# Two attention layers in a fused kernel: score maxima run twelve steps ahead of the exponentials, not sixteen

## The chip, the cores and the metric

One core of one Trainium2 chip runs the whole program. The metric is device time in microseconds (us), from a few executions. Below, TensorE is PE in the rows, VectorE DVE, ScalarE ACT, GpSimd POOL, and SyncE SP. SP issues nearly all the DMAs of the layers concerned.

## The reference, cut to what matters

Eight sequences (batches) of 512 tokens, width 256, go through eight layers: four attention layers and four routed expert layers, each added to its input. Two of the attention layers are changed, "rope" (the second) and "latent" (the fourth). Both are 16-head attention with head size 16 and rotary embedding:

```
q = q * cos + rotate_half(q) * sin
k = k * cos + rotate_half(k) * sin
scores = einsum('bqhd,bkhd->bhqk', q, k) * scale
attn = softmax(scores, axis=-1)
out = einsum('bhqk,bkhd->bqhd', attn, v)
return out.reshape(b, l, d) @ Wo
```

In rope q, k and v come from one projection; in latent k and v go through a width of 128, and q is the normalised input itself.

## The kernel before, in words

Both layers are built by one function, `mha_pairs` (line 2001), over the whole layer's batches (NB = 8). The softmax needs each row's maximum before it can take exponentials, and the exponentials are made on scores that are laid out the other way round (keys on the partitions). So every score is computed twice: once as "top" (`max_scores`, line 2282), from which VectorE takes row maxima (`maxima`, line 2497), and once as "exp" (`exp_scores`, line 2296), from which ScalarE takes exponentials (line 2426). The maxima of a group of four heads are split into two 16-bit rows each, turned (`split_maxima`, line 2505), written by SP to DRAM (`write_rows`, line 2206) and loaded back as two extra rows of the query tile (`load_rows`, line 2213). The exp matmul of that group contracts over them too, and so subtracts the maximum. These loads are called the *row loads* here.

A batch is 32 steps u, in four groups of 8 (`grp = u // 8`). A step holds one exp score tile and one top score tile of 128 x 1024 each; the top tile of step u belongs to the step 16 later (`top_of`, line 2033). Sixteen top tiles are made alone before the loop (lines 2334 and 2567), and the last sixteen steps have exp tiles only. Both kinds share three PSUM slots in one fixed order (line 2038); a tile's matmuls wait until the tile three places before it is read (`wait_slot`, line 2110). So the exp tile of step n waits for the maxima that VectorE takes in step n - 2, and for the first of a group TensorE also waits for its row loads (line 2300).

Beside this, TensorE runs the probability-value products (`value_sums`, line 2309) every second step and, at the steps of `USES` (line 2013), one of the projections, transposes and output products. VectorE rotates k and q of the next batch at steps 2, 4, 16 and 18 (`ROTATE_AT`, `rotate`), normalises heads after steps 4, 12, 20 and 28 and adds the output after 8 and 10. Each rotation starts a chain of five operations on GpSimd (lines 2619 to 2622) that ends with the low part of the 16-bit split; then SP may write the parts to DRAM (`write_parts`, line 2186). After two such writes SP loads half of the next batch's keys and queries (`load_half`, line 2195).

SP works through one hand-written order (lines 2230 to 2249): an item that waits blocks all items behind it. Batch b's order before is: row write and load of group 1; parts 0; row write 2; parts 1; row load 2; half 0; row write and load 3; parts 2; parts 3; row write of the next batch's group 0; half 1; its row load.

VectorE splits and turns a group's maxima at steps 0, 8, 16 and 24, for the group that begins eight steps later (line 2581).

```
if top_of(b, u) is not None:
    maxima(top_of(b, u))
if u % 8 == 0 and b * 4 + u // 8 + 1 < NB * 4:
    split_maxima(*divmod(b * 4 + u // 8 + 1, 4))
if b + 1 < NB and u in ROTATE_AT:
    rotate(b + 1, ROTATE_AT.index(u))
```

Of the kernel before, what the change touches and what calls it, by code (L numbers as in the profile page):

```python
# [13 lines left out]
NB, S, D = 8, 512, 256  # L14
# [1986 lines left out]
def mha_pairs(nc, g, ins, project_q, biased, results):  # L2001
# [3 lines left out]
    FIRST = results.first_batch  # L2005
    READY = 4 * max(FIRST, 1)
    late_rows, late_results = results.capacity, not results.capacity
    STEPS, NM = 32, 8
    XN = 4 if project_q else 8
    RAISE = 1.0 if project_q else Q_RAISE  # L2010
    KQ_TOP = 8.0 if project_q else 4.0 / Q_RAISE
# [14 lines left out]
    def uses_at(b, u):  # L2026

        return [(name, b + OF_BATCH[name]) for at, name in USES if at == u and 0 <= b + OF_BATCH[name] < NB]
# [3 lines left out]

    def top_of(b, u):

        n = b * STEPS + u + 16
        return n if n < NB * STEPS else None

    scores = [("top", n) for n in range(16)]
    for n in range(NB * STEPS):
        scores += [("exp", n)] + ([("top", n + 16)] if n + 16 < NB * STEPS else [])  # L2040
    place = {x: i for i, x in enumerate(scores)}
    CHAINS = [(o, c) for c in range(2) for o in "kq"]

    with ExitStack() as ctx:
# [53 lines left out]
        def rows_of(nb, o, c):  # L2098

            return scr[(nb * 2 + "kq".index(o)) * 2 + c]  # L2100
# [16 lines left out]
        def heads_of(grp, hp):  # L2117

            return grp // 2, 2 * (grp % 2) + hp
# [37 lines left out]
        def normalise(eng, nb, t):  # L2157
            i = nb * 4 + t
            if project_q:
                eng.tensor_scalar(xn[:, t, :], X[:, i, :], MV[:, i, 0:1], RSTD[:, 0, i:i + 1], ALU.subtract,  # L2160
                                  ALU.mult).then_inc(xn_ready, 1)
                return
            for c in range(2):
                half = slice(c * P, (c + 1) * P)
                eng.tensor_scalar(xn[:, t, half].rearrange("p (a y h) -> p h y a", a=8, y=2),
                                  X[:, i, half].rearrange("p (h y a) -> p h y a", y=2, a=8), MV[:, i, 0:1],
                                  RSTD[:, 0, i:i + 1], ALU.subtract, ALU.mult).then_inc(xn_ready, 1)
# [3 lines left out]
        @block.sync  # L2171
        def _(sp):
            if late_rows:
                results.load(sp, 0)
            for name, src in ins["load"]:
                sp.dma_start(tiles[name][:], src).then_inc(loaded_by[name], 16)
            if late_rows:
                for q in range(1, NB):
                    results.load(sp, q)

            sp.wait_ge(level_set, 1)
            for y in range(2):
                sp.dma_start(KS[64 * y + 48:64 * y + 50, :, :, :, :].rearrange("r b c l s -> r (b c l) s"),
                             level[:, :].unsqueeze(1).to_broadcast([2, 16, S])).then_inc(level_spread, 16)

            def write_parts(nb, j):

                o, c = CHAINS[j]
                sp.wait_ge(low_done, nb * 4 + j + 1)
                rows = rows_of(nb, o, c).rearrange("(j d) (h t) -> (d h) j t", d=16, h=8)  # L2190
                for first, n, i in ((0, 2, 0), (2, 1, 1)) if o == "k" else ((1, 2, 0), (0, 1, 1)):
                    sp.dma_start(rows[:, first:first + n, :], parts[:, j, i:i + 1, :].to_broadcast([P, n, S])).then_inc(
                        parts_written[j], 16)

            def load_half(nb, c):

                for j in (2 * c, 2 * c + 1):
                    sp.wait_ge(parts_written[j], 32 * (nb + 1))
                if nb >= 2:
                    sp.wait_ge(b_ready, (nb - 2) * STEPS + 16 * (c + 1))  # L2200
                for o, to in (("k", KS), ("q", QS)):
                    for y in range(2):
                        sp.dma_start(to[64 * y:64 * y + 48, nb % 2, c, :, :].rearrange("r l s -> r (l s)"),
                                     rows_of(nb, o, c)[:, 4 * y * S:(4 * y + 4) * S]).then_inc(half_loaded[c], 16)

            def write_rows(nb, grp):

                n = nb * 4 + grp
                sp.wait_ge(rows_turned, n + 1)
                sp.dma_start(rowscr[n].rearrange("a b -> (a b)").rearrange("(r q i) -> q r i", q=4, i=32),  # L2210
                             mpT[:, n % 2, :]).then_inc(rows_written[n % 2], 16)

            def load_rows(nb, grp):

                n = nb * 4 + grp
                c, at = heads_of(grp, 0)
                sp.wait_ge(rows_written[n % 2], 16 * (n // 2 + 1))
                for y in range(2):
                    sp.dma_start(QS[64 * y + 48:64 * y + 50, nb % 2, c, at:at + 2, :],
                                 rowscr[n][4 * y:4 * y + 4, :]).then_inc(rows_loaded[grp], 16)  # L2220

            for c in range(2):
                for j in (2 * c, 2 * c + 1):
                    write_parts(0, j)
                load_half(0, c)
            for grp in range(1):
                write_rows(0, grp)
                load_rows(0, grp)

            for b in range(NB):  # L2230
                more = b + 1 < NB
                write_rows(b, 1)
                load_rows(b, 1)
                if more:
                    write_parts(b + 1, 0)
                write_rows(b, 2)
                if more:
                    write_parts(b + 1, 1)
                load_rows(b, 2)
                if more:  # L2240
                    load_half(b + 1, 0)
                write_rows(b, 3)
                load_rows(b, 3)
                if more:
                    write_parts(b + 1, 2)
                    write_parts(b + 1, 3)
                    write_rows(b + 1, 0)
                    load_half(b + 1, 1)
                    load_rows(b + 1, 0)

        @block.tensor
        def _(pe):
# [29 lines left out]
            def max_scores(n):  # L2282

                nb, (grp, a) = n // STEPS, divmod(n % STEPS, NM)
                if grp % 2 == 0 and a == 0:
                    pe.wait_ge(half_loaded[grp // 2], 64 * (nb + 1))
                wait_slot(pe, "top", n)
                qt, hp = divmod(a, 2)
                c, l = heads_of(grp, hp)
                for y in range(2):  # L2290
                    rows = slice(64 * y, 64 * y + 48)
                    last = pe.matmul(psS[:, slot_of("top", n), y, :], QS[rows, nb % 2, c, l, qt * P:(qt + 1) * P],  # L2292
                                     KS[rows, nb % 2, c, l, :], start=True, stop=True)
                last.then_inc(a_ready, 1)
# [36 lines left out]
                    pe.wait_ge(loaded_by[f"w{name[0]}"], 16)  # L2331
                work(name, nb)
            pe.wait_ge(scales_ready, 1)
            for n in range(16):
                max_scores(n)
            pe.wait_ge(ones_set, 2)
            pe.wait_ge(level_spread, 32)
# [102 lines left out]
        def _(dve):  # L2440
# [56 lines left out]
            def maxima(n):  # L2497
                nb, (grp, a) = n // STEPS, divmod(n % STEPS, NM)
                dve.wait_ge(a_ready, n + 1)
                if a == 0 and nb * 4 + grp >= 2:  # L2500
                    dve.wait_ge(split_done, 2 * (nb * 4 + grp - 1))
                qt, hp = divmod(a, 2)
                dve.tensor_reduce(mx[:, grp % 2, :, hp, qt], psS[:, slot_of("top", n), :, :], AX.X, ALU.max).then_inc(a_done, 1)  # L2503
# [60 lines left out]
            dve.wait_ge(m_ready, turn["xT1", 0] + 1)  # L2564
            for t in range(4):
                normalise(dve, 1, t)
            for n in range(16):
                maxima(n)
                if n == 7:
                    split_maxima(0, 0)  # L2570
# [3 lines left out]
            for b in range(NB):  # L2574
                for u in range(STEPS):
                    for name, nb in uses_at(b, u - 1) if u else uses_at(b - 1, STEPS - 1):
                        if name[:2] in TURNED_BY_DVE:
                            (normalise_heads if name[:2] == "OT" else add_out)(nb, int(name[-1]))
                    if top_of(b, u) is not None:
                        maxima(top_of(b, u))  # L2580
                    if u % 8 == 0 and b * 4 + u // 8 + 1 < NB * 4:
                        split_maxima(*divmod(b * 4 + u // 8 + 1, 4))
                    if b + 1 < NB and u in ROTATE_AT:
                        rotate(b + 1, ROTATE_AT.index(u))
# [358 lines left out]
def hybrid_stack(nc, w, out):  # L2943

    with ExitStack() as ctx:
# [25 lines left out]
        with layer("experts1"):  # L2971
            routed_layer(nc, g, experts_a, False, then=lambda results: named(
                "rope", mha_pairs, rope, True, False, results))
# [84 lines left out]
```

## Time and profile before

| | us |
|---|---|
| median of 3 runs | 2870.66 |
| lowest and highest | 2863.97, 2878.41 |
| profiled execution, its own time | 2863.06 |
| its span, first to last instruction | 2861.3 |
| TensorE busy | 2315.3 (81%) |
| VectorE busy | 1942.5 (68%) |
| ScalarE busy | 1535.4 (54%) |
| rope layer, first top tile to last exponential | about 946 to 1410 |
| latent layer, first exp tile to last | about 2133 to 2566 |
| mean granted TensorE clock | 0.904 |

Busy shares are means over layers with different limits. In the rows a time on the left is the start in us from the start of the span, the next number a duration; "idle before <- releaser" in brackets is how long the engine stood idle and what ended it. A granted clock of 1.00 is 2.4 GHz, 0.50 is 1.2 GHz.

### The profile page before, as it was taken

The page shows a single profiled execution, that of the slowest core. Times are in us where ns is not written, and L with a number is a line of the kernel's source. Part 1 is how long each engine was busy: PE and PEld are TensorE (multiplying, and loading weights), DVE is VectorE, ACT ScalarE, POOL GpSimd, SP SyncE. Part 2 cuts the span into 40 slices and gives each one's busy share as a digit, 9 for nine tenths or more (in the row PEclk, how much of TensorE's full clock was granted, in tenths as well). Part 3 has the DMA queues.
Part 4 walks back from the last instruction along what each step waited for, and adds up shares of the span by engine and source line. Part 5 has one row for each costly group of instructions (what it writes and reads, how often), then busy time and mean ns, then how long its engine had stood idle before and what let it go on. Part 6 is the DMA issues. An engine that isn't in the chain of part 4 may idle for free. (4 is left out here: it accounts for less than half of the span.)

```text
span 2861.3 us, 40653 instructions
## 1 busy us (share of the span) xinstructions
PE 2315.3 (81%) x13550; PEld 1159.4 (41%) x13550; DVE 1942.5 (68%) x4549; ACT 1535.4 (54%) x2426; POOL 911.8 (32%) x851
## 2 busy tenths in 40 slices
PE   4799999999666799999757688389859999984698
PEld 2334444443453233333246455256522333323465
DVE  5788888887535888888462444577568888864343
ACT  2477676777623477777652333255427777772122
POOL 0232223330134244543024300435416545413211
PEclk7799999999887799999888899589959999996899
DMA  7565565651145121212016100556242121204242
GB/s 243 183 183 181 176 196 172 191 178 40 61 158 170 46 68 46 68 48 66 25 71 204 60 1 1 174 214 224 97 121 68 52 63 52 62 24 149 94 148 74
DMA packets 193506, 318.32 MB, mean 111 GB/s; under 512 B 29285, under 2 KB 155272, under 8 KB 188564
## 3 DMA queue, kind: packets, MB, share of 16 engines
q1 hardware_dynamic: 177764, 266.31, 29.8%
q0 software_dynamic: 15536, 49.41, 5.1%
q8 instruction: 111, 1.82, 0.3%
q14 instruction: 95, 0.78, 0.1%
HBM read 164.41 MB, written 151.59 MB: 110 GB/s over the span
## 5 line engine op out<-in xcount | busy, mean ns | idle before, releaser
L1816 DVE CUSTOM_DVE_ANT_0 decay_junk<-decay_scores_q,decay_corr 128x512 bf16<-128x512 f32 x512 | 338.3, 685 | 110.4 <-PE decay_scores_q L1553 108.7
L1733 ACT ACTIVATE decay_probs<-decay_scores_k 128x512 f32<-128x512 f32 x512 | 294.4, 597 | 189.3 <-PE decay_scores_k L1572 154.1
L2426 ACT ACTIVATE latent_probs<-latent_scores,latent_escale 128x1024 f32<-128x1024 f32 x256 | 281.8, 1115 | 137.0 <-PE latent_scores L2305 135.8
L2426 ACT ACTIVATE rope_probs<-rope_scores,rope_escale 128x1024 f32<-128x1024 f32 x256 | 282.6, 1115 | 133.3 <-PE rope_scores L2305 131.9
L2503 DVE TENSOR_REDUCE rope_mx<-rope_scores 128x2 f32<-128x1024 f32 x256 | 308.6, 1222 | 57.6 <-PE rope_scores L2292 56.1
L2503 DVE TENSOR_REDUCE latent_mx<-latent_scores 128x2 f32<-128x1024 f32 x256 | 307.9, 1221 | 53.3 <-PE latent_scores L2292 52.6
L1553 PE MATMUL decay_scores_q<-decay_KS,decay_QS 96*128 96x512 bf16 x512 | 204.2, 400 | 35.3 <-DVE decay_mx L1816 23.4
L1569 PE MATMUL decay_scores_k<-decay_QS,decay_KS 99*128 99x384 bf16 (+3 forms) x512 | 156.8, 307 | 14.9 <-DMA decay_QS<-decay_mT 7.2
L2318 PE MATMUL latent_out_heads<-latent_probs,latent_Vaug 128*32 128x512 f32 x1024 | 140.7, 622 | 6.7 <-ACT latent_Osb L2417 4.1
L2318 PE MATMUL rope_out_heads<-rope_probs,rope_Vaug 128*32 128x512 f32 x1024 | 138.1, 612 | 5.9 <-ACT rope_Osb L2417 4.1
L1597 PE MATMUL decay_out_heads<-decay_probs,decay_Vaug 128*32 128x512 f32 x1024 | 141.5, 626 | 0.8 <-DVE decay_probs L1828 0.8
L2292 PE MATMUL latent_scores<-latent_KS,latent_QS 48*128 48x512 f16 x512 | 102.7, 400 | 32.9 <-ACT latent_probs L2426 18.9
L208 PE MATMUL experts_logits_results<-experts_we,experts_xT 128*128 x384 | 116.9, 434 | 12.5 <-DVE experts_y L348 4.6
L1569 PEld LDWEIGHTS decay_scores_k<-decay_QS,decay_KS 99*128 99x128 bf16 x512 | 49.3, 97 | 177.5 <-issue 87.6
L2292 PE MATMUL rope_scores<-rope_KS,rope_QS 48*128 48x512 f16 x512 | 101.5, 395 | 19.6 <-DVE rope_mx L2503 7.9
L348 DVE TENSOR_TENSOR experts_y<-experts_logits_results,experts_be 128x256 f32<-128x256 f32 x96 | 39.7, 424 | 107.0 <-PE experts_logits_results L208 68.6
L2305 PE MATMUL latent_scores<-latent_QS,latent_KS 50*128 50x512 f16 x512 | 101.2, 394 | 12.2 <-DVE latent_mx L2503 12.1
L2127 POOL TENSOR_TENSOR rope_fc<-rope_f,rope_tab 128x512 f32<-128x512 f32 x28 | 35.8, 1277 | 234.9 <-DVE rope_sh L2495 234.9
L58 POOL DMA_INDIRECT dispatched<-experts_XN,experts_slot x64 | 62.5, 976 | 143.8 <-DVE experts_slot L337 99.9
L2305 PE MATMUL rope_scores<-rope_QS,rope_KS 50*128 50x512 f16 x512 | 100.0, 390 | 8.6 <-DVE rope_mx L2503 8.4
L765 ACT ACTIVATE experts4x_hT<-experts4x_inner 128x512 f16<-128x512 f32 x64 | 38.2, 597 | 125.3 <-PE experts4x_inner L669 125.3
L1572 PE MATMUL decay_scores_k<-decay_QS,decay_KS 99*128 99x256 bf16 (+2 forms) x384 | 105.0, 274 | 0.0
(455 smaller groups left out, 5138.2 us busy)
## 6 DMA issues: line engine op xcount, KB each, us to landing
decay_KS<-decay_parts_dram SPq DMA_DIRECT2D x64, 384.0 KB
decay_QS<-decay_parts_dram SPq DMA_DIRECT2D x64, 384.0 KB
decay_parts_dram<-decay_parts SPq DMA_DIRECT2D x56, 384.0 KB, 3.1
experts3x_w<-in_w_dram SPq DMA_DIRECT2D x16, 1024.0 KB, 10.9
weight_parts<-experts3x_w SPq DMA_DIRECT2D x8, 2048.0 KB, 7.7
experts4x_w<-weight_parts SPq DMA_DIRECT2D x8, 2048.0 KB, 8.0
decay_parts_dram<-decay_parts SPq DMA_DIRECT2D x56, 256.0 KB, 3.3
experts_xin<-dispatched SPq DMA_DIRECT2D x96, 128.0 KB
```

Of the source, the lines that this page charges most:

```text
L208: last = pe.matmul(psL[:, n % 2, 0:D], xT[:, n % 2, c, :], we[:, c, bass.ds(at, D)], start=(c == 0), stop=(c == 1))
L1553: pe.matmul(psA[:, A_BANK[k], :], QS[0:96, 0, c, hh, qt * P:(qt + 1) * P], KS[0:96, NV - 1, c, hh, :], start=True, stop=True).then_inc(a_r ...
L1569: last = pe.matmul(psB[:, s % 2, 0:end], KS[:, 1, c, hh, keys], QS[:, 0, c, hh, 0:end], start=True, stop=True)
L1572: last = pe.matmul(psB[:, s % 2, end:S], KS[:, 0, c, hh, keys], QS[:, 1, c, hh, end:S], start=True, stop=True)
L1597: last = pe.matmul(psO[32 * h:32 * h + 32, :], Vaug[:, b % 2, kt, 4 * grp + h, :], probs[:, (b * 16 + kk) % PSLOTS, h, :], start=(kt == 0) ...
L1733: act.activation(probs[:, (b * 16 + kk) % PSLOTS, h, :], psB[:, s % 2, :], ACT.Exp, scale=scale).then_inc(exp_done, 1)
L1816: dve.tensor_tensor_reduce(junk[:, a % 2, :], psA[:, A_BANK[k], :], corr[:, qt, :], 1.0, -3.0e38, ALU.mult, ALU.max, mx[:, grp % 2, qt, h: ...
L2292: last = pe.matmul(psS[:, slot_of("top", n), y, :], QS[rows, nb % 2, c, l, qt * P:(qt + 1) * P], KS[rows, nb % 2, c, l, :], start=True, st ...
L2305: last = pe.matmul(psS[:, slot_of("exp", b * STEPS + u), y, :], KS[rows, b % 2, c, l, kt * P:(kt + 1) * P], QS[rows, b % 2, c, l, :], star ...
L2318: last = pe.matmul(psO[32 * h:32 * h + 32, :], Vaug[:, b % 2, kt, 4 * grp + h, :], probs[:, kk % 2, h, :], start=(kt == 0), stop=(kt == 3))
L2426: act.activation(probs[:, kk % 2, 2 * (u % 2):2 * (u % 2) + 2, :], psS[:, slot_of("exp", n), :, :], ACT.Exp, scale=escale[:, 0:1]).then_in ...
L2503: dve.tensor_reduce(mx[:, grp % 2, :, hp, qt], psS[:, slot_of("top", n), :, :], AX.X, ALU.max).then_inc(a_done, 1)
```

## The change

It replaces the sixteen by `LEAD = 12` in the order of the tiles, in the prologue of both TensorE and VectorE and in `top_of`. It moves `split_maxima` from steps 0, 8, 16, 24 to steps 4, 12, 20, 28, still for the group that begins next, now four steps later instead of eight. And it changes SP's order: parts 0, parts 1 and half 0 now stand between row load 1 and row write 2; parts 2 stands between row load 2 and row write 3; parts 3 between row write 3 and row load 3; half 1 ahead of the next batch's row write 0.

```diff
-    STEPS, NM = 32, 8
+    STEPS, NM, LEAD = 32, 8, 12
...
-        n = b * STEPS + u + 16
+        n = b * STEPS + u + LEAD
...
-    scores = [("top", n) for n in range(16)]
+    scores = [("top", n) for n in range(LEAD)]
...
-        scores += [("exp", n)] + ([("top", n + 16)] if n + 16 < NB * STEPS else [])
+        scores += [("exp", n)] + ([("top", n + LEAD)] if n + LEAD < NB * STEPS else [])
...
                 load_rows(b, 1)
                 if more:
                     write_parts(b + 1, 0)
+                    write_parts(b + 1, 1)
+                    load_half(b + 1, 0)
                 write_rows(b, 2)
-                if more:
-                    write_parts(b + 1, 1)
                 load_rows(b, 2)
                 if more:
-                    load_half(b + 1, 0)
+                    write_parts(b + 1, 2)
                 write_rows(b, 3)
+                if more:
+                    write_parts(b + 1, 3)
                 load_rows(b, 3)
                 if more:
-                    write_parts(b + 1, 2)
-                    write_parts(b + 1, 3)
+                    load_half(b + 1, 1)
                     write_rows(b + 1, 0)
-                    load_half(b + 1, 1)
                     load_rows(b + 1, 0)
...
-            for n in range(16):
+            for n in range(LEAD):
                 max_scores(n)
...
-            for n in range(16):
+            for n in range(LEAD):
                 maxima(n)
...
-                    if u % 8 == 0 and b * 4 + u // 8 + 1 < NB * 4:
+                    if u % 8 == 4 and b * 4 + u // 8 + 1 < NB * 4:
                         split_maxima(*divmod(b * 4 + u // 8 + 1, 4))
```

## Rows read from the trace of the kernel before

**Rows 1.** The page, part 1 (busy us and share) and one group of part 5.
```profile
PE 2315.3 (81%) x13550; PEld 1159.4 (41%) x13550; DVE 1942.5 (68%) x4549; ACT 1535.4 (54%) x2426; POOL 911.8 (32%) x851
...
L2503 DVE TENSOR_REDUCE rope_mx<-rope_scores 128x2 f32<-128x1024 f32 x256 | 308.6, 1222 | 57.6 <-PE rope_scores L2292 56.1
```
**Rows 2.** Stretches: PE, PEld, DVE, ACT, POOL busy, clock, DMA. Rope's second batch.
```profile
1020.06:1076.94 56.88, 54.86 (x340) 18.99 (x336) 49.01 (x73) 42.02 (x47) 26.95 (x24) 1.00 0.20 58
```
**Rows 3.** Timeline of rope's prologue: row load 0, last top tile, first exp tile.
```profile
958.18 0.52 SPq L2219 DMA_DIRECT2D rope_QS<-rope_tops_dram  x2
...
961.85 0.61 PE L2292 MATMUL rope_scores<-rope_KS,rope_QS 48*128 48x512 f16 x2 [0.52 <-DVE rope_mx L2503]
...
963.07 0.61 PE L2305 MATMUL rope_scores<-rope_QS,rope_KS 50*128 50x512 f16 x2 [0.61 <-DVE rope_mx L2503]
```
**Rows 4.** Timeline of rope's last batch: exp tiles of steps 0, 16 and 24.
```profile
1361.18 0.39 PE L2305 MATMUL rope_scores<-rope_QS,rope_KS 50*128 50x512 f16 x2
...
1387.65 0.60 PE L2305 MATMUL rope_scores<-rope_QS,rope_KS 50*128 50x512 f16 x4
...
1397.25 0.60 PE L2305 MATMUL rope_scores<-rope_QS,rope_KS 50*128 50x512 f16 x4
```
**Rows 5.** Timeline of SP, rope's third batch from step 16.
```profile
1109.03 0.52 SPq L2210 DMA_DIRECT2D rope_tops_dram<-rope_mpT  x1
1110.95 0.52 SPq L2219 DMA_DIRECT2D rope_QS<-rope_tops_dram  x2
1115.62 6.66 SPq L2192 DMA_DIRECT2D rope_parts_dram<-rope_parts  x4
```
**Rows 6.** Timeline of VectorE, the same: split, rotation; after the maxima of steps 20 and 28.
```profile
1108.38 0.17 DVE L2512 TENSOR_SCALAR rope_mp<-rope_mx 128x16 f16<-128x16 f32 x1
...
1108.93 0.72 DVE L2495 STREAM_SHUFFLE rope_sh<-rope_f 128x512 f32<-128x512 f32 x1
...
1116.58 0.25 DVE L2524 RECIPROCAL rope_rec<-rope_work 128x16 f32<-128x16 f32 x1
...
1129.67 0.25 DVE L2524 RECIPROCAL rope_rec<-rope_work 128x16 f32<-128x16 f32 x1
```
**Rows 7.** Timeline of GpSimd, the same: the last operation of chain 3.
```profile
1120.22 1.15 POOL L2148 TENSOR_TENSOR rope_parts<-rope_fc,rope_parts 128x512 f16<-128x512 f32 x1
```
**Rows 8.** Timeline of TensorE, the same: exp tiles of steps 24 and, next batch, 0.
```profile
1120.74 0.39 PE L2305 MATMUL rope_scores<-rope_QS,rope_KS 50*128 50x512 f16 x2
...
1133.83 0.39 PE L2305 MATMUL rope_scores<-rope_QS,rope_KS 50*128 50x512 f16 x2
```
**Rows 9.** Latent's third batch: rotation at step 16, chain 3's end, exp tile of step 24.
```profile
2277.89 0.74 DVE L2495 STREAM_SHUFFLE latent_sh<-latent_f 128x512 f32<-128x512 f32 x1
...
2289.18 1.16 POOL L2148 TENSOR_TENSOR latent_parts<-latent_fc,latent_parts 128x512 f16<-128x512 f32 x1
...
2288.55 0.39 PE L2305 MATMUL latent_scores<-latent_QS,latent_KS 50*128 50x512 f16 x2
```
**Rows 10.** DMA issues by line: size and median us from issue to landing.
```profile
rope_KS<-rope_parts_dram SPq DMA_DIRECT2D x32, 192.0 KB, 3.2
rope_QS<-rope_parts_dram SPq DMA_DIRECT2D x32, 192.0 KB, 4.1
```
**Rows 11.** Timelines of SP and TensorE, rope's third batch: half 0; exp tile of step 7.
```profile
1098.62 0.88 SPq L2203 DMA_DIRECT2D rope_QS<-rope_parts_dram  x2
...
1089.35 0.39 PE L2305 MATMUL rope_scores<-rope_QS,rope_KS 50*128 50x512 f16 x2 [0.16 <-DVE rope_mx L2503]
```
**Rows 12.** Busy time in stretches of latent: group 1 of two batches; two adjacent stretches.
```profile
2202.33:2220.07 17.74, 16.34 (x92) 5.83 (x89) 15.18 (x26) 9.77 (x11) 13.42 (x14) 0.90 0.35 90
2259.38:2275.54 16.16, 14.76 (x92) 5.65 (x89) 14.96 (x26) 9.76 (x11) 13.89 (x14) 1.00 0.32 99
2210.20:2213.60 3.40, 2.00 (x20) 0.81 (x20) 3.30 (x8) 1.50 (x3) 3.40 (x5) 1.00 0.85 189
2213.60:2217.10 3.50, 3.50 (x13) 0.67 (x12) 2.91 (x5) 2.01 (x2) 2.44 (x2) 0.51 0.25 46
```

## The prediction

> **What bounds the kernel now.** I read the page's busy times first, then the busy times by stretch, then the timelines of one batch, engine by engine. TensorE is busy 81% of the span, VectorE 68% [rows 1], but these are means over eight layers. In a middle batch of the rope layer TensorE is busy 54.86 of 56.88 us, with VectorE at 49.01 and ScalarE at 42.02 [rows 2]. So inside these loops TensorE is the bound, with some 2 us per batch to spare, and an idle TensorE is not made up for later. A step is 56.88 / 32 = 1.78 us. The row loads never show as a wait, because a group's maxima are split eight steps, some 14 us, before they are needed. The change takes four of these eight steps away; the question is what is left of that reserve, and what stands in SP's queue meanwhile.
>
> **Prologue and end.** The first exp tile starts at 963.07, 1.2 us after the last top tile [rows 3]. Four top tiles fewer would let it start some 4 x 1.2 = 4.9 us earlier, at about 958.2. But row load 0 is issued at 958.18 [rows 3], and its split does not move. How long such a load takes to land no row shows. The write of the same kind takes from 1109.03 to 1110.95, 1.92 us, since SP issues the load as soon as the write is down [rows 5]; the far end is the 192 KB load at 3.2 us [rows 10]. A row load (two DMAs of 4 KB by the code) is nearer to the write of 8 KB: I take 1.9 us, and keep 3.2 for the range. So the first exp tile starts at 960.1: 3.0 us gained. The number of exp tiles does not change, but four more of them have a top tile beside them and four fewer have none. In the last batch the paired steps take (1387.65 - 1361.18) / 16 = 1.65 us, the unpaired ones (1397.25 - 1387.65) / 8 = 1.20 us [rows 4]: 4 x 0.45 = 1.8 us lost. Per layer the shorter lead gives 1.2 us, both layers 2.4 us. That is all it can give while TensorE is the bound.
>
> **Row load 3 behind parts 3.** This is the largest term. In the new order SP issues row write 3 (split at step 20), then must wait for chain 3 on GpSimd before it may issue parts 3, and only then issues row load 3, which TensorE needs at step 24.
> Rope: chain 3 ends at 1120.22 + 1.15 = 1121.37 [rows 7], 12.44 us after the shuffle that starts chain 2 [rows 6]. Step 16 has no split any more, so that shuffle starts 0.55 us earlier (1108.93 - 1108.38, rows 6), and chain 3 ends at 1120.8. The two DMAs of parts 3 keep SP for 0.9 us: four DMAs and the wait between them end at 1115.62 + 6.66 = 1122.28 [rows 5], 0.9 after the chain. Row load 3 is issued at 1121.7 and lands 1.9 us later at 1123.6. The exp tile of step 24 started at 1120.74 [rows 8]: TensorE stands 2.9 us. Its write is not the problem: the maxima of step 20 end at about 1116.6 [rows 6], the split at 1117.3, the write is down at 1119.2.
> Latent: the same chains end at 2290.34 after a shuffle at 2277.89, and step 24 starts at 2288.55 [rows 9]. With the 0.55: 2289.8 + 0.9 + 1.9 = 2292.6, a stall of 4.05 us.
> Seven batches of each layer have a next batch, thus a chain 3: 7 x 2.9 + 7 x 4.05 = 48.7 us. Behind TensorE's wait stand its top tile, the value products and v1, so VectorE and ScalarE run dry too, and nothing is caught up.
>
> **The other row loads.** For group 0 of the next batch: the maxima of step 28 end at about 1129.75 [rows 6], a split is 0.63 us, so 1130.4; write 1.92, load 1.9, issue some 0.05: 1134.25 against 1133.83 [rows 8], 0.4 us late. Group 2 has about 0.4 us more room and comes to 0.1. Group 1 is covered by the next term. That is 0.5 x 14 = 7.0 us.
>
> **Splits on VectorE.** At step 4 VectorE already has a rotation and then the heads, and step 7 starts with TensorE waiting for it [rows 11]. A 0.6 us split there delays the tile of step 7 by that. The split taken away from step 8 would give it back, but the output addition behind it has to wait for TensorE anyway, which is now late. I take 0.6 x 14 = 8.4 us; the ends are 0 and 0.6. This delay covers group 1's row load (needed 3.9 us after its split, there with 4.1). At steps 12 and 20 TensorE and the late load hide the split, at 28 the row load does.
>
> **TensorE's clock.** In latent's second batch, a stretch with 2.00 of 3.40 us busy at clock 1.00 (2.4 GHz) is followed by one at 0.51 (1.2 GHz). Its group took 17.74 us, the same group of the next batch at full clock 16.16 [rows 12]: 1.58 us for one such fall. Idle of 2.9 or 4.05 us in one piece leaves TensorE less busy than those 2.00 us, and what follows at step 24 is a full step (v1). I take one fall for each stall: 1.6 x 14 = 22.4 us. The low end is 0.
> The Trainium skill, "TensorE: Matmul & The Clock Gate" (section "Why this matters for your kernels"), says that long idle gaps between bursts of matmuls drop the clock to half. By it the falls come; without it, by the busy share alone, the sum would be 22.4 us less.
>
> **The rest.** Half loads, parts 0 and 1, and normalising on GpSimd keep their producers; the first top tile of a half comes four steps later than before, so those loads gain room: 0. No instruction is added or removed, and no bytes.
>
> **The sum.** 2863.1 - 6.0 + 3.6 + 48.7 + 7.0 + 8.4 + 22.4 = 2947.2 us against the profiled execution's own 2863.06. The median of the runs shown lies 7.6 us above that execution, so I forecast 2955 us, 84 us or 2.9% slower. Some 0.5% is what a measurement of this kernel can tell from no change.
>
> **Rivals.**
> *The clock holds.* Stalls as above, but no falls. For it: between falls, latent's loop dips below full use elsewhere and keeps 1.00 [rows 12]. Against: none of those dips is a stall of 3 us. 2955 - 22 = 2933 us.
> *A queue behind the halves.* Half 0 now stands close ahead of row write 2. Its last load is issued at about 1099.1 [rows 11] and lands 4.1 us later [rows 10], at 1103.2; row write 2 is issued at 1102.8. If the small write's packets had to wait behind the half, at the most some 1.6 us would be added per batch and TensorE waits for that at step 16: 1.6 x 14 = 22 us, 2977 us. Against: most of the data is gone by then.
> The Trainium skill, "DMA: Bandwidth & Descriptors" (section "Queues, rings and completion order"), says that each DMA engine takes the descriptors of a ring in their order. That is this mechanism; no run here shows a row write behind a half.
> *The load is slow.* If it lands after 3.2 us, all four groups are late by 1.0 to 1.3 us more: 4.9 x 14 = 69 us, 3024 us. Against: that is the time of 48 times the bytes.
> *The reserve covers it.* Four steps are some 7 us; write and load are 3.9. If chain 3 ended before the maxima of step 20 (1116.6), parts 3 would be gone and row load 3 not blocked; TensorE would meet no wait, and step 8, where VectorE is crowded by output additions, would be rid of its split: 14 x 0.63 = 8.8 us gained, with the 2.4 above 11.2 us, so 2859 us. It decides from the point at which row load 3 lands before step 24 begins; by the rows it misses that by 2.9 and 4.05 us. For it speaks only a chain that is faster than the rows show.
>
> **How the numbers follow.** Forecast 0.60, clock holds 0.20, queue behind halves 0.08, slow load 0.05, reserve covers 0.07 (of it 0.02 beyond 0.5%). Faster 0.02, same 0.05, slower 0.93. The range: below, the clock holds (2933), the crowding costs nothing (-8), the small late loads are on time (-7) and and a few us more of the stalls made up for or the loads down sooner: 2908. Above, the queue case (2977) with the shuffle of step 16 no earlier (0.55 x 14 = 8): 2985. That leaves out the last two rivals, 0.12, and a little at the edges.
>
> **What would show it.** In the timeline of SP, row load 3 right behind parts 3, at 1121.7 or its like, every batch; in the waits, TensorE's exp tiles released by the DMA of the row loads, 7 x 2.9 us in rope and 7 x 4.05 in latent, and small ones for the other groups. By stretches, batches of some 62.5 us in rope, and a clock of 0.5 after step 24. The last batch of each layer should have no large stall. Wrong it would be if row load 3 is issued before parts 3's wait ends, if exp tiles of step 24 are not late, or if most of the loss lies at steps 8, 16 or 32.

## The result, and the profile after

| | before | changed |
|---|---|---|
| median of 4 runs, us | 2870.43 | 2941.51 |
| lowest to highest | 2863.97 to 2878.41 | 2939.09 to 2949.31 |
| profiled execution's span | 2861.3 | 2947.6 |

The ratio is 1.0251, with a 95% interval of 1.0219 to 1.0283: 2.5% slower. The forecast was 2955 us, with a range of 2908 to 2985. Measured again for the experiments below, the ratio was 1.0271 (1.0245 to 1.0297).

The profiled executions differ by 86.3 us of span, more than the medians' 71.1 us: the change's was the slowest of its four, and that of the kernel before lay 7.4 us under its median. Between the first top tile and the last exponential of a layer, rope went from 464.6 to 507.1 us and latent from 461.0 (2115.2 to 2576.2; its last exp tile starts at 2573.6, not at the about 2566 of the table of before) to 504.6: 86.1 us together, so all of it lies in the two layers.

Busy times of the changed kernel, the page's part 1, as in [rows 1]:

```profile
PE 2341.4 (79%) x13550; PEld 1169.4 (40%) x13550; DVE 1956.3 (66%) x4549; ACT 1536.6 (52%) x2426; POOL 911.8 (31%) x851
```

Instruction counts are the same. TensorE and VectorE show more busy time for the same work: matmuls at the lower clock, and stretched splits (the two split operations take 17.5 us more in the two layers together).

The waits of rope's stretch and of latent's (what waited, for what: us in total, times, longest), changed kernel:

```profile
PEld rope_scores L2305 <- DMA rope_QS<-rope_tops_dram: 44.7, 30, 3.3
PE rope_scores L2305 <- DMA rope_QS<-rope_tops_dram: 20.0, 12, 2.4
...
PEld latent_scores L2305 <- DMA latent_QS<-latent_tops_dram: 44.5, 29, 3.6
```

Before, neither layer had one such line. A weight load waits a little longer than the matmul behind it, so the first line is not all TensorE idle; the second, 20.0 us, is; in latent the same is 16.9 us, 13 times. Now nearly every group's first exp tile is released by its row load.

The four groups of the third batch of each layer, in the columns of [rows 2]. First the kernel before, rope and then latent:

```profile
1076.94:1090.98 14.04, 13.78 (x84) 3.98 (x80) 11.63 (x18) 10.60 (x13) 7.16 (x7) 1.00 0.06 17
1090.98:1106.59 15.61, 14.72 (x92) 5.66 (x89) 14.55 (x26) 9.77 (x11) 8.75 (x8) 1.00 0.32 88
1106.59:1120.74 14.15, 13.80 (x88) 4.85 (x84) 12.08 (x18) 11.05 (x14) 10.42 (x10) 1.00 0.10 31
1120.74:1133.83 13.09, 12.57 (x88) 4.53 (x85) 10.77 (x14) 10.62 (x13) 0.64 (x1) 1.00 0.36 91
...
2275.54:2288.55 13.01, 11.81 (x84) 4.21 (x81) 11.86 (x18) 10.53 (x13) 9.34 (x9) 1.00 0.11 33
2288.55:2301.64 13.09, 12.57 (x88) 4.52 (x85) 10.77 (x14) 10.62 (x13) 1.71 (x2) 1.00 0.34 93
```

The changed kernel, the same groups:

```profile
1086.25:1101.22 14.97, 13.75 (x80) 3.96 (x80) 12.02 (x18) 10.50 (x13) 8.04 (x7) 1.00 0.04 13
1101.22:1116.79 15.57, 14.80 (x94) 5.72 (x90) 14.21 (x26) 9.87 (x12) 7.84 (x7) 1.00 0.38 92
1116.79:1133.89 17.10, 13.83 (x88) 4.77 (x86) 12.98 (x18) 11.27 (x14) 11.05 (x10) 0.97 0.15 48
1133.89:1149.75 15.86, 15.37 (x84) 5.61 (x85) 10.22 (x13) 10.51 (x12) 0.00 (x0) 0.82 0.20 51
...
2331.14:2348.21 17.07, 12.80 (x84) 4.17 (x81) 13.80 (x18) 10.76 (x13) 11.03 (x10) 0.89 0.15 48
2348.21:2362.92 14.71, 14.19 (x85) 5.32 (x86) 10.24 (x13) 10.53 (x12) 0.00 (x0) 0.89 0.27 56
```

Rope's group 0 is 0.93 us longer, its group 1 unchanged. Group 2, which ends where step 24 begins, is 2.95 us longer in rope and 4.06 in latent. Group 3 is 2.77 and 1.62 us longer, at a mean clock of 0.82 and 0.89. In latent the clock is down to 0.89 already in group 2, ahead of step 24. Over the seven batches with a next one, group 3 averages 15.25 us in rope and 14.98 in latent. Rope's batches with a next one took 62.5 to 63.7 us; some 62.5 was forecast.

The timelines of SP and TensorE at this place of the changed kernel, beside [rows 5, 8]:

```profile
1125.26 0.90 SPq L2192 DMA_DIRECT2D rope_parts_dram<-rope_parts  x2
1128.21 0.52 SPq L2210 DMA_DIRECT2D rope_tops_dram<-rope_mpT  x1
1131.05 0.88 SPq L2192 DMA_DIRECT2D rope_parts_dram<-rope_parts  x2
1131.97 0.60 SPq L2219 DMA_DIRECT2D rope_QS<-rope_tops_dram  x2
...
1133.89 0.61 PE L2305 MATMUL rope_scores<-rope_QS,rope_KS 50*128 50x512 f16 x2 [2.31 <-DMA rope_QS<-rope_tops_dram]
...
1134.86 3.78 PE L2278 MATMUL rope_work<-rope_wv,rope_xnT 128*128 128x256 f32 x8
```

Row write 3 goes out at 1128.21. Its load could follow 1.9 us later, but SP stands before parts 3 until 1131.05, and row load 3 leaves at 1131.97. The exp tile starts 1.92 us after that, 2.31 us of idle TensorE behind it, and then v1's eight matmuls take 3.78 us at half clock.

### The profile page after: what moved, and what is told of

Read it like the earlier page. It is cut to its first block and busy times, and to the rows that moved or that the text cites. A ratio compares the mean times of both kernels' runs of the same rounds, so it can differ in the third digit from the quotient of the medians.

```text
span 2947.6 us, 40654 instructions
## 1 busy us (share of the span) xinstructions
PE 2341.4 (79%) x13550; PEld 1169.4 (40%) x13550; DVE 1956.3 (66%) x4549; ACT 1536.6 (52%) x2426; POOL 911.8 (31%) x851
## 5 line engine op out<-in xcount | busy, mean ns | idle before, releaser
L2305 PE MATMUL latent_scores<-latent_QS,latent_KS 50*128 50x512 f16 x512 | 103.5, 403 | 33.2 <-DMA latent_QS<-latent_tops_dram 16.9
L1569 PEld LDWEIGHTS decay_scores_k<-decay_QS,decay_KS 99*128 99x128 bf16 x512 | 49.5, 97 | 175.8 <-issue 86.1
L58 POOL DMA_INDIRECT dispatched<-experts_XN,experts_slot x64 | 62.5, 976 | 144.2 <-DVE experts_slot L337 100.2
```

The lines of the kernel that those rows point to most:

```text
L1569: last = pe.matmul(psB[:, s % 2, 0:end], KS[:, 1, c, hh, keys], QS[:, 0, c, hh, 0:end], start=True, stop=True)
L2305: last = pe.matmul(psS[:, slot_of("exp", b * STEPS + u), y, :], KS[rows, b % 2, c, l, kt * P:(kt + 1) * P], QS[rows, b % 2, c, l, :], star ...
```

## The experiments

Ratios are to runs of the kernel before on the same chip, with 95% intervals. One kernel, the one with TensorE kept busy, was measured on two chips and came out at 1.0253 and 1.0207. So ratios of different chips that differ by 0.5% or less are not told apart here.

### Row load 3 first

```diff
                 write_rows(b, 3)
+                load_rows(b, 3)
                 if more:
                     write_parts(b + 1, 3)
-                load_rows(b, 3)
-                if more:
                     load_half(b + 1, 1)
```

> The changed kernel with one line moved: row load 3 stands ahead of parts 3 in SP's order again. Theory (order): the stall of TensorE at step 24 and the clock falls behind it go (48.7 + 22 us in the prediction), what stays are the late small loads, the crowded split at step 4 and the 2.4 us gained: 0 to 20 us above the kernel before, ratio 1.000 to 1.007, and no half clock inside the loops beyond those of before. Rival (reserve): four steps are too short for write and load whatever stands between them, so most of the loss stays: ratio above 1.015.

Measured: 1.0108 (1.0086 to 1.0129), median 2888.6 against 2857.5. More than half of the loss is gone, and more stays (31 us) than the 0 to 20 expected. The same four groups of rope in this kernel:

```profile
1076.08:1091.04 14.96, 13.74 (x80) 3.96 (x80) 11.90 (x18) 10.38 (x13) 8.04 (x7) 1.00 0.04 13
...
1106.60:1121.65 15.05, 13.83 (x89) 4.78 (x86) 12.64 (x18) 11.11 (x14) 11.06 (x10) 1.00 0.09 29
1121.65:1134.92 13.27, 12.71 (x84) 4.51 (x85) 10.64 (x14) 10.76 (x13) 0.00 (x0) 1.00 0.31 90
```

Group 3 is back to 13.27 us and clock 1.00. Groups 0 and 2 keep 0.9 us each; latent's group 2 keeps 1.8 us (14.8 against 13.01). The exp tile of step 24 is still released by its row load, but idle before it is 0.25 us, not 2.31:

```profile
1121.65 0.39 PE L2304 MATMUL rope_scores<-rope_QS,rope_KS 50*128 50x512 f16 x2 [0.25 <-DMA rope_QS<-rope_tops_dram]
```

### The order alone

The kernel before with the changed order of SP and nothing else; its edit is the third part of the diff shown above the prediction.

> The kernel before (lead sixteen, splits at steps 0, 8, 16, 24) with the changed order of SP alone. Theory (order): row load 3 is issued only after parts 3, at 1122.3 in rope's third batch, lands 1.9 us later at 1124.2 against 1120.7, and in latent 4.6 us late: 7 x (3.5 + 4.6) = 57 us, with a clock fall for each of the 14 some 22 to 35 us more: 79 to 92 us slower, ratio about 1.03, although the lead is the old one. Rival (reserve): the shorter lead is what costs, the order alone costs nothing: ratio 1.000 to 1.003.

Measured: 1.0316 (1.0292 to 1.0340), 88 us by the medians. At lead sixteen, too, the order alone costs about as much as the whole change (71 and 77 us in its two measurements); whether more is not shown, since they were not taken beside it. Group 2 is 3.5 us longer in rope and 4.7 in latent, on average of the seven batches. SP's timeline and TensorE's first exp tile of step 24, rope's third batch:

```profile
1130.15 0.52 SPq L2210 DMA_DIRECT2D rope_tops_dram<-rope_mpT  x1
1133.92 0.88 SPq L2192 DMA_DIRECT2D rope_parts_dram<-rope_parts  x2
1134.84 0.61 SPq L2219 DMA_DIRECT2D rope_QS<-rope_tops_dram  x2
...
1136.73 0.61 PE L2305 MATMUL rope_scores<-rope_QS,rope_KS 50*128 50x512 f16 x2 [3.40 <-DMA rope_QS<-rope_tops_dram]
```

The load leaves 0.9 us after the chain's end, as in the change, and TensorE idles 3.40 us (forecast for this kernel 3.5). The idle is longer than the change's 2.31 for two reasons of equal size: the work before it ends 0.57 us earlier in its group, without a stretched split at step 20, and the load leaves 0.55 us later, behind the split at step 16.

### The order of before under the change

The changed kernel with SP's old order back.

> The changed kernel (lead twelve, splits at 4, 12, 20, 28) with SP's order of before. Row load 3 is free; but row load 0 of the next batch now stands right behind half 1 while its split is at step 28. If small loads pass the half's data they land 1.9 us after their issue: 0.8 us late at step 0, in all 10 to 30 us over the kernel before. If they wait behind the half (4.1 us to landing) TensorE stands some 3 us at step 0 of seven batches of both layers, with clock falls: 60 to 85 us over the kernel before, as slow as the change itself.

Measured: 1.0373 (1.0344 to 1.0402), 103 us, over the upper expectation. The blocked item is now row load 0, behind half 1. SP and TensorE, rope, step 32:

```profile
1144.08 0.89 SPq L2203 DMA_DIRECT2D rope_QS<-rope_parts_dram  x2
1145.01 0.57 SPq L2219 DMA_DIRECT2D rope_QS<-rope_tops_dram  x2
...
1148.95 0.61 PE L2305 MATMUL rope_scores<-rope_QS,rope_KS 50*128 50x512 f16 x2 [2.83 <-DMA rope_QS<-rope_tops_dram]
```

The tile starts 3.94 us after the load's issue. In all fourteen such places of this kernel it is 3.4 to 4.7 us, and where TensorE waited for a row load with no half in front, 1.7 to 2.0 us. So the small load does wait for something of the half in front. A shorter lead with this order of before is slow too, and needs a new one: the question was which.

### TensorE kept busy in the stall

```diff
             def exp_scores(b, u):
...
+                if u == 24 and b + 1 < NB:
+                    pe.wait_ge(m_taken, turn["v1", b + 1])
+                    for _ in range(5):
+                        pe.matmul(psM[:, 0:D], ident[:, :], wv[:, 0, :], start=True, stop=True)
                 if u % 8 == 0:
                     pe.wait_ge(rows_loaded[grp], 32 * (b + 1))
```

> The changed kernel with five extra 128x256 matmuls (f32, into the free work bank, overwritten by v1) ahead of TensorE's wait for row load 3, in the seven batches with a next one: some 2.1 us of work inside a stall of 2.3 to 4 us, so the load lands no later and the stall takes as long, but TensorE is not idle. Theory (clock): the falls to 1.2 GHz behind step 24 go and with them 14 x 1.6 to 2.5 us: 22 to 35 us faster than the changed kernel, ratio to before about 1.013 to 1.018. Rival (clock costs nothing, the stall is all): as the changed kernel, ratio 1.025.

Measured: 1.0253 (1.0226 to 1.0280), above the expected 1.013 to 1.018 and no better than the change's 1.0251, though that one was not taken beside it. So both kernels ran once more beside each other:

> The changed kernel as it is, once more, beside the next one on the same chip: 1.022 to 1.030 times the kernel before.

> The kernel of e5_kept_busy once more. In its profile the clock stayed at 1.00 behind step 24 in rope, and rope and latent together took 19 us less than in the changed kernel, but its ratio to the kernel before came out the same as the change's, measured on another chip. Theory (the falls cost some 1.5 us each): 15 to 25 us, 0.5 to 0.9%, faster than the changed kernel beside it. Rival: no difference beyond 0.3%.

Measured: the change 1.0271 (1.0245 to 1.0297), median 2941.39; kept busy 1.0207 (1.0180 to 1.0234), median 2925.77. Five useless matmuls per batch make it 15.6 us, 0.5%, faster. Groups 2 and 3 of rope's third batch, first the kept-busy kernel, then the change beside it:

```profile
1115.99:1133.60 17.61, 16.19 (x98) 6.59 (x96) 12.97 (x18) 11.26 (x14) 11.04 (x10) 1.00 0.14 47
1133.60:1146.75 13.15, 12.70 (x85) 4.51 (x84) 10.17 (x13) 10.46 (x12) 0.00 (x0) 1.00 0.23 62
```

```profile
1117.50:1134.56 17.06, 13.83 (x88) 4.77 (x85) 12.98 (x18) 11.27 (x14) 11.04 (x10) 1.00 0.15 49
1134.56:1149.55 14.99, 14.39 (x84) 5.60 (x85) 10.32 (x13) 10.62 (x12) 0.00 (x0) 0.89 0.21 54
```

Group 2 is as long as in the change and 0.55 us more, since the extra matmuls end a little after the load. Group 3 drops from 14.99 to 13.15 us and stays at 2.4 GHz. That the clock falls cost time beside the stall is thereby shown. With 0.55 us for every stall they come to 15.6 + 14 x 0.55 = 23 us, or 1.7 us for each. Group 3 by itself, over all batches of the two traces, is 2.2 us shorter in rope and 1.7 in latent: 27 us.

In latent the filled stall did not keep the clock up everywhere. It stayed behind step 24, but inside group 2 it fell in four of seven batches, as here, and such a group took 18.5 us instead of 17.4:

```profile
2373.75:2392.21 18.46, 15.72 (x94) 6.46 (x91) 13.81 (x18) 10.75 (x13) 11.03 (x10) 0.91 0.16 53
```

### Splits one step earlier

`u % 8 == 3` in place of `== 4`, on top of "row load 3 first".

> e1_load3_first with each split one step earlier (steps 3, 11, 19, 27, right behind the group's last maxima). In e1 groups 0 and 2 of a batch kept 0.9 and 1.0 us over the kernel before. If that is the late load (0.4 us), it goes: ratio about 1.003. If it is VectorE, which has the split beside GpSimd's chain and the rotation, then a step earlier changes little, since the chain runs at steps 3 and 19 too: it stays at 1.007 to 1.011, with the splits still stretched to 0.6 to 1.2 us.

Measured: 1.0068 (1.0040 to 1.0096). It lies between the two expectations, and its interval overlaps that of "row load 3 first" (another chip), so the two are not told apart. Latent's group 2 was 14.4 us instead of 14.8, rope's 16.3 instead of 15.05 in its third batch, with the clock at 0.96. There the split of step 19 fell beside two of GpSimd's operations: its two first operations, 0.17 us each in [rows 6], took 1.13 and 1.21 us. A step earlier moves the load's date and the crowd together. By the two traces it took 12.7 us out of latent and added 6.9 to rope.

### The splits' place with the old lead

Lead sixteen, splits at steps 4, 12, 20, 28, SP's order of "row load 3 first".

> Lead sixteen as before, with the splits at steps 4, 12, 20, 28 and the order of e1_load3_first. Theory: what e1 keeps comes from where the splits stand, not from the shorter lead, so this one is as slow as e1: 1.008 to 1.012, and its loop steps as long as e1's. Rival: the lead of twelve itself costs (less distance between maxima and exponentials): then this one is at 1.000 to 1.004.

Measured: 1.0111 (1.0079 to 1.0144), against 1.0108 for lead twelve on another chip. Group by group it is the same loop, rope's third batch:

```profile
1080.02:1094.99 14.97, 13.75 (x81) 3.99 (x82) 11.96 (x18) 10.45 (x13) 8.05 (x7) 1.00 0.04 13
...
1110.55:1125.61 15.06, 13.84 (x89) 4.78 (x86) 12.65 (x18) 11.11 (x14) 11.07 (x10) 1.00 0.09 29
1125.61:1138.85 13.24, 12.71 (x85) 4.51 (x86) 10.60 (x14) 10.73 (x13) 0.00 (x0) 1.00 0.30 90
```

So what "row load 3 first" keeps does not come from the distance between maxima and exponentials. It comes with the splits at steps 4 and 20 and the late row loads that follow from them; these two were not separated.

### One split out of the crowd

The kernel before with group 2's split alone moved:

```diff
-                    if u % 8 == 0 and b * 4 + u // 8 + 1 < NB * 4:
+                    if u in (0, 12, 16, 24) and b * 4 + u // 8 + 1 < NB * 4:
```

> The kernel before (lead sixteen, splits at 0, 16, 24) with group 2's split alone moved from step 8 to step 12, and SP's order to match: parts 1 and half 0 ahead of row write 2, nothing between row write and row load. Theory (a split costs where VectorE is the bound or beside GpSimd's chain, and nothing where TensorE is): steps 8 to 13, with two output additions, lose a split of 0.6 to 1.2 us, and the split lands ahead of k1's projection: 0.3 to 0.6 us per batch less, and perhaps latent's clock falls behind step 13: 4 to 13 us, 0.1 to 0.5%, faster than the kernel before. Rival (row load 2 behind half 0 lands late, or the crowd only moves): 1.000 to 1.003.

Measured over 12 runs: 0.9995 (0.9978 to 1.0011), no difference; the expectation of a gain is not borne out. Rope's group 1:

```profile
1092.10:1107.87 15.77, 14.80 (x94) 5.67 (x90) 14.33 (x26) 9.77 (x11) 8.72 (x8) 1.00 0.35 87
```

It is 0.16 us longer than before, although VectorE is 0.22 us less busy. Latent's second to seventh batches took 55.5 to 55.8 us where every second one had taken 57.1 or more: the clock did not fall in them. That is some 5 us. Against it, latent's first batch was 2.0 us longer, and rope's first 4.1: there row write 2 was issued 0.5 us behind half 0 and took 3.9 us, TensorE stood 2.06 us for row load 2, and its next projection ran at half clock. So the rival's first condition did occur, in one batch of rope. No kernel of the study beats the one before.

## Why the prediction was right, point by point

**Prologue: right. End: not shown.** From the first top tile to the first exp tile rope took 17.36 us before and 14.36 after: 3.0 gained. The row load sets that start, as forecast:

```profile
959.14 0.52 SPq L2219 DMA_DIRECT2D rope_QS<-rope_tops_dram  x2
...
961.02 0.61 PE L2305 MATMUL rope_scores<-rope_QS,rope_KS 50*128 50x512 f16 x2 [2.13 <-DMA rope_QS<-rope_tops_dram]
```

It is 1.88 us from issue to tile; 1.9 was taken. The whole last batch of rope, with its end, grew by 2.3 us (forecast 1.8), that of latent by 0.6. But with the lead of sixteen in all of them, this last batch took 49.2 us in the kernel before, 46.3 in "the order alone" and 50.1 in "the splits' place with the old lead", so a loss of 1.8 us can't be read from it.

**Row load 3 behind parts 3: the mechanism and the date right, its marginal worth too high.** The exp tile of step 24 came 2.95 and 4.06 us later in its group (forecast 2.9 and 4.05), which confirms the walk from the shuffle through GpSimd's chain, SP's two issues and the landing. But 48.7 us is not what this order costs on top of the rest of the change. "Row load 3 first" takes out 0.0143 to 0.0163 (from the change's two ratios, not taken beside it) of some 2865 us, 41 to 47 us, stalls and clock falls together. Group by group, against the change's trace, it shortens group 2 by 1.9 us per batch (rope) and 2.1 (latent) and group 3 by 2.0 and 1.6: 28 us of stalls and 25 us behind them. The rest of the delay was there anyway, hidden behind the late load: without it group 2 still has 0.9 us (rope) and 1.8 (latent) too much. At lead sixteen nothing hides there, and "the order alone" pays 3.5 and 4.7 us per batch, the 57 us that were expected of it. The step that mis-sized it is "At steps 12 and 20 TensorE and the late load hide the split". It was true of the sum and wrong as an account: a term that hides behind another still has to be paid when that one is removed.

**Splits on VectorE, and the other row loads: too small.** Forecast 8.4 + 7.0 = 15.4 us; "row load 3 first" has both and the gain of the lead and is 31 us slow. Step 4's delay was 0.9 us per batch in rope and 0.45 in latent (0.6 taken). At step 20 a split of 0.6 us was assumed, but beside GpSimd's chain it took 1.4 us in rope and 2.3 in latent. The timeline of latent's third batch of the changed kernel, VectorE and then GpSimd:

```profile
2339.99 0.86 DVE L2512 TENSOR_SCALAR latent_mp<-latent_mx 128x16 f16<-128x16 f32 x1
2340.89 1.20 DVE L2514 SCALAR_TENSOR_TENSOR latent_mp<-latent_mx,latent_mp 128x16 f16<-128x16 f32 x1
...
2339.55 1.28 POOL L2127 TENSOR_TENSOR latent_fc<-latent_xnT,latent_tab 128x512 f32<-128x512 f32 x1
2340.78 1.28 POOL L2132 TENSOR_TENSOR latent_sh<-latent_sh,latent_tab 128x512 f32<-128x512 f32 x1
```

The first ends at 2340.85, with GpSimd's first at 2340.83; the second at 2342.09, with GpSimd's second at 2342.06. The split read before the prediction [rows 6] stood where GpSimd was idle. The trace of before held the warning all the same, at a split of latent's step 8 that no row shows:

```profile
2204.12 1.15 DVE L2512 TENSOR_SCALAR latent_mp<-latent_mx 128x16 f16<-128x16 f32 x1
```

Not all of the 31 us is the splits' own. In "row load 3 first" latent's second and sixth batches are 7.6 and 4.3 us longer than before, more than any other. In the second the moved work brought a tiny copy of VectorE beside a large operation of GpSimd, in the sixth a split, which took 2.33 us; TensorE then stood, and the clock fell. VectorE and GpSimd of that kernel, second batch:

```profile
2222.91 2.16 DVE L2544 COPY X<-latent_mv 128x4 f32<-128x4 f32 x1
...
2222.70 2.34 POOL L2602 TENSOR_TENSOR X<-X,latent_xb 128x1024 f32<-128x1024 f32 x1
```

Row load 0 at step 32, on the other hand, cost less than the 0.4 us taken: with TensorE kept busy, rope's group 3 has 13.15 us against 13.09.

**The clock: the total right, the picture right in rope alone.** Forecast one fall per stall at 1.6 us, 22.4 us; measured 23 to 27 us in all. In rope TensorE idled 2.3 to 2.4 us at each of the seven stalls, and the clock fell each time; with that idle filled, it stayed each time. One fall was not one price: rope's group 3 took 14.6 to 14.8 us four times (mean clock 0.88 or 0.89) and 15.9 to 16.0 us three times (0.81 or 0.82). In latent the stall was not 4.05 us of idle in one piece. The delay of the third batch is spread over three waits, and the clock was down before the last:

```profile
2342.99 0.66 PE L2272 MATMUL latent_work<-ident_sb,latent_attn 128*128 128x128 f32 x4 [1.20 <-DVE latent_attn L2526]
...
2344.73 1.94 PE L2318 MATMUL latent_out_heads<-latent_probs,latent_Vaug 128*32 128x512 f32 x8
```

Between these two rows TensorE idled 0.48 us for the maxima, and after them 1.54 us for the row load. The sums at 2344.73 take 1.94 us where they take 1.07 at full clock. In latent's seventh batch TensorE idled 2.48 us for row load 3 and the clock did not fall. What a fall costs is shown; which idle brings it on, in latent, is not. The Trainium skill, "TensorE: Matmul & The Clock Gate" (section "Why this matters for your kernels"), says that long idle gaps between bursts of matmuls drop the clock to half. Rope's trace agrees, with 2.3 us; latent's falls came after shorter gaps as well.

**The sum.** 84.1 us were forecast for the profiled execution and 86.3 found; the medians moved 71.1 us, and 77.2 when measured again. The terms make a good total partly by compensation, which is luck: order and clock 71 forecast and 41 to 53 found; splits and small loads, less the lead's gain, 13 forecast and 31 found.

**The rivals.** "The reserve covers it" is refuted by every wait shown. "The load is slow" as well: 1.65 to 2.1 us from issue to tile with no half in front. "The clock holds" did not. "A queue behind the halves" is a real mechanism, but in thirteen of the change's fourteen batches not at that place: row write 2 was down after 1.9 to 2.2 us, since it stood mostly 3 us or more behind the half. Rope's third batch:

```profile
1107.92 0.89 SPq L2203 DMA_DIRECT2D rope_QS<-rope_parts_dram  x2
1112.71 0.53 SPq L2210 DMA_DIRECT2D rope_tops_dram<-rope_mpT  x1
1114.64 0.52 SPq L2219 DMA_DIRECT2D rope_QS<-rope_tops_dram  x2
```

In rope's first batch it stood 1.6 us behind, took 3.25 us, and TensorE idled 0.84 us for row load 2. In "the order alone", where the same write is issued right behind the half, it took 4.5 us, and 2.8 to 4.7 in all batches:

```profile
1111.15 0.89 SPq L2203 DMA_DIRECT2D rope_QS<-rope_parts_dram  x2
1112.08 0.53 SPq L2210 DMA_DIRECT2D rope_tops_dram<-rope_mpT  x1
1116.59 0.52 SPq L2219 DMA_DIRECT2D rope_QS<-rope_tops_dram  x2
```

The rule of the Trainium skill, "DMA: Bandwidth & Descriptors" (section "Queues, rings and completion order"), that each DMA engine takes the descriptors of a ring in their order, agrees with this and with row load 0 in "the order of before under the change".

## What to carry to other kernels

When a lead is shortened, walk the queue that feeds the consumer item by item, with the time at which each item's own wait ends: one late producer in front of an urgent load costs more than the shorter lead can give, and the gain of a shorter lead is only the unpaired steps at both ends. An idle bound engine may pay twice, once for the stall and once for the clock behind it. A tiny operation on the way to an urgent load is priced by what runs beside it. And a term that is hidden behind a bigger one is to be written down with its own price, since it is what remains when the bigger one is repaired.

## What the runs showed of the hardware that was not expected

Tiny VectorE operations that turn 32-bit maxima into 16-bit rows take 0.17 us alone. Beside GpSimd's two-input operations on 128x512 or 128x1024 they took 0.22 to 2.33 us, and ended 0.02 to 0.04 us after them, as if they waited for them to finish. That holds in all 287 cases of the eleven traces where the GpSimd operation had begun before and had more than 0.18 us to go. The price is thus what is left of GpSimd's current operation: up to 1.24 us beside one of 1.28, up to 2.33 beside one of 2.36. Beside GpSimd's one-input operations they took at most 0.5 us. The reductions over PSUM (1.22 us; 625.4 us in all in the two layers before, 625.1 changed) and the turning (0.21 us in all cases) did not stretch beside either. The Trainium skill, "SBUF — State Buffer" (section "Who interferes with whom"), says that VectorE and GpSimd share one pair of ports that is held for a whole instruction, that a tensor-scalar operation in a two-port mode or one with two inputs from SBUF needs it, and that a reduction does not. The traces agree with it in all three beside the two-input operations; which mode the tensor-scalar operation ran in no run shows, nor why GpSimd's one-input operations held it up so little.

A DMA of 4 or 8 KB on SP's queue takes 1.65 to 2.1 us when nothing big is in front, read from its issue to the item that waited for it. Issued 0.5 to 0.8 us behind the last of four loads of 192 KB, a row load took 3.4 to 4.7 us and a row write 2.8 to 4.7; in the change, some 3 us or more behind them, row write 2 took 1.9 to 2.0.
